# A fused attention and feed-forward block: smaller constant loads, a halved first weight load and another engine for one scaling at the start

## What is computed

```python
x = x + tanh(g_xattn[0]) * xattn(layernorm(x), ctx_2048, ...)
x = x + tanh(g_ffn[0]) * ffn(layernorm(x), ...)

# xattn: 16 query heads, 4 key/value heads of 128
q = rms_norm(x @ wq, q_norm_w)
k = rms_norm(x @ wk, k_norm_w);          v = x @ wv
k_ctx = rms_norm(h_ctx_kv @ wk_ctx, k_norm_w);  v_ctx = h_ctx_kv @ wv_ctx
q = q * cos + rotate_half(q) * sin       # k likewise, k_ctx not
scores = q @ concat([k_ctx, k]).T / sqrt(128) + causal mask on the own keys
out = softmax(scores) @ concat([v_ctx, v]) @ wo
# ffn: silu(x @ gate_w * gate_scale) * (x @ up_w * up_scale) @ down_w * down_scale,
#      weights rounded through float8_e4m3
```

## Time and profile before

| | |
|---|---|
| time before, median of 3 runs | 309.91 us (309.84 to 309.98) |
| the profiled execution | 310.24 us |
| its span in the profile | 308.0 us |
| TensorE / VectorE / ScalarE / GpSimd busy | 294.0 / 231.3 / 232.1 / 183.4 us |
| moved by DMA | 12.84 MB, most of it in the first 31 us |
| TensorE clock granted | full in all 40 slices |

### The profile page before, as it was taken

How to read it: one execution, slowest core, us unless ns; L and a number is a source line. 1 busy time by engine, 2 the same in 40 slices (tenths; PEclk the granted TensorE clock), 3 DMA queues, 4 the chain that set the end, 5 groups by cost and what they waited for, 6 DMA issues and landing times.

```text
span 308.0 us, 6587 instructions
## 1 busy us (share of the span) xinstructions
PE 294.0 (95%) x2243; PEld 235.3 (76%) x2243; DVE 231.3 (75%) x482; ACT 232.1 (75%) x893; POOL 183.4 (60%) x178
## 2 busy tenths in 40 slices
PE   7898989998999999999999999999999999988876
PEld 3345666666877888888888888888888888877865
DVE  1768997899899987879864876768765975686553
ACT  2586889977879788998887778787887678776632
POOL 1446685677648695567755685457746684556230
PEclk9999999999999999999999999999999999999999
DMA  6999000000000010001000010000000000000001
GB/s 198 388 390 397 24 17 2 0 1 10 11 3 1 2 34 2 0 2 36 2 0 2 0 37 0 3 0 20 2 1 2 0 19 2 2 0 19 0 0 36
DMA packets 6720, 12.84 MB, mean 42 GB/s; under 512 B 800, under 2 KB 4256, under 8 KB 6688
## 3 DMA queue, kind: packets, MB, share of 16 engines
q1 hardware_dynamic: 6688, 12.43, 11.3%
HBM read 11.38 MB, written 1.05 MB: 40 GB/s over the span
## 4 chain that ended last, share of the span: by engine, by line
PE 28%; ACT 28%; DVE 26%; issue 8%; POOL 5%; DMA 2%; SPq 1%; DVEq 0%; POOLq 0%
ACT probs L950 11%; ACT squares L785 6%; PE ps_y L446 4%; DVE row_max L1245 4%; DVE exp_bias L1248 4%; DVE q_sin L1109 4%; DVE q_rot L1105 3%; ACT qt L869 3%; PE ps_attn L752 3%; PE ps_scores L704 3%; ACT const L842 2%; PE ps_transposed L432 2%; PE ps_kv L420 2%; DMA q_raw<-in_wq_dram 2%; PE ps_probs L432 2%
## 5 line engine op out<-in xcount | busy, mean ns | idle before, releaser
L950 ACT ACTIVATE probs<-ps_scores,exp_bias,q_scale 128x128 f32<-128x128 f32 x128 | 56.9, 455 | 23.7 <-DVE exp_bias L1248 23.6
L1426 POOL TENSOR_TENSOR q_rot<-q_rot,q_sin 128x512 f32<-128x512 f32 x31 | 40.0, 1292 | 18.4 <-DVE q_sin L1109 18.1
L1470 POOL TENSOR_TENSOR probs<-probs,row_inv 128x512 f32<-128x512 f32 x32 | 36.2, 1133 | 17.9 <-DVE row_inv L1304 17.8
L1377 POOL TENSOR_TENSOR q_scale<-ssq_eps,minus_half 128x4 f32<-128x4 f32 x32 | 39.8, 1244 | 10.6 <-DVE ssq_eps L1274 9.6
L1388 POOL TENSOR_TENSOR fuse_lo<-fuse,fuse_hi 128x256 fp32r<-128x256 f32 x21 | 15.4, 733 | 41.3 <-ACT fuse_hi L794 41.3
L785 ACT ACTIVATE squares<-ps_q 128x128 bf16<-128x128 f32 x128 | 34.1, 292 | 5.8 <-PE ps_q L414 4.1
L752 PE MATMUL ps_attn<-pt,values 128*128 128x256 f32 x128 | 33.4, 383 | 0.0
L704 PE MATMUL ps_scores<-kt,qt 128*64 128x128 f32 x512 | 33.3, 273 | 0.0
L926 ACT ACTIVATE pt<-ps_probs 128x512 f32<-128x512 f32 x32 | 19.2, 600 | 13.3 <-PE ps_probs L432 13.3
L704 PEld LDWEIGHTS ps_scores<-kt,qt 128*64 128x64 f32 x512 | 28.9, 137 | 0.0
L1105 DVE TENSOR_TENSOR q_rot<-ps_q,rope 128x512 f32<-128x512 f32 x31 | 21.3, 686 | 9.7 <-ACT squares L785 9.7
(11 more groups left out here) (195 smaller groups left out, 839.2 us busy)
## 6 DMA issues: line engine op xcount, KB each, us to landing
q_raw<-in_wq_dram SPq DMA_DIRECT2D x4, 512.0 KB, 8.3
o_raw<-in_wo_dram SPq DMA_DIRECT2D x4, 512.0 KB, 12.3
ctx_t<-in_ctx_dram SPq DMA_DIRECT2D x8, 128.0 KB, 2.7
out_dram<-x_sb SPq DMA_DIRECT2D x8, 128.0 KB, 1.7
stage<-in_gate_w_dram SPq DMA_DIRECT2D x2, 384.0 KB, 10.1
stage<-in_up_w_dram SPq DMA_DIRECT2D x2, 384.0 KB, 11.1
x_sb<-in_x_dram SPq DMA_DIRECT2D x1, 768.0 KB, 13.1
stage<-in_down_w_dram SPq DMA_DIRECT2D x2, 384.0 KB, 13.1
```

The source lines that it names most:

```text
L950: last = nc.scalar.activation(probs[:, i, :], ps_s[:, i * P:(i + 1) * P], ACT.Exp, bias=exp_bias[:, i:i + 1], scale=q_scale[:, k % 2, i:i ...
L1377: return nc.gpsimd.tensor_tensor(dst, src, minus_half[:, 0:src.shape[1]], ALU.pow)
L1426: nc.gpsimd.tensor_tensor(q_rot[:, :, :], q_rot[:, :, :], q_sin[:, :, :], ALU.add)\
L1470: nc.gpsimd.tensor_tensor(probs[:, :, :], probs[:, :, :], row_inv[:, :].unsqueeze(2).broadcast_to([P, 4, P]), ALU.mult).then_inc(probs_rea ...
```

## The change

Six edits, all in what is done before step 0:

1. The norm weights come as two rows of 128 (`norm_w`, 128 KB over all partitions, where it was 256 KB). The swapped halves are read by an access pattern when the rope tables are made.
2. The causal mask moves from the table ahead of `q` 0 (160 KB before, 128 KB now) into `small` (7.5 KB before, 39.5 KB now), which is loaded after `q` 0. `mask_tables` waits for `small`.
3. The first weight chunk, `wk_ctx`, is loaded in two halves of 256 KB with a semaphore each, so one more DMA is issued. TensorE waits for the first half, multiplies with it, waits for the second and multiplies with that.
4. The first gate chunk is issued ahead of the fourth query chunk.
5. ScalarE scales the context keys, one instruction for each of four heads with the head's inverse root as a scale column, after the squares of the own keys. VectorE's one instruction for it is gone.
6. The own keys' inverse roots have a tile of their own, `own_inv`. GpSimd no longer waits for the scaled context keys before it writes them.

```diff
-C_COS, C_SIN, C_MASK, C_ID, C_ALL = 0, DIM, 2 * DIM, 2 * DIM + LEN, 2 * DIM + LEN + P
-S_KW, S_GATES, S_GATE, S_UP, S_ALL = 0, 1, 3, 3 + FC, 3 + 2 * FC
+C_COS, C_SIN, C_ID, C_ALL = 0, DIM, 2 * DIM, 2 * DIM + P
+S_KW, S_GATES, S_GATE, S_UP, S_MASK, S_ALL = 0, 1, 3, 3 + FC, 3 + 2 * FC, 3 + 2 * FC + LEN
...
-CHUNKS = [("kv", 0), ("kv", 1), ("q", 0), ("kv", 2), ("kv", 3), ("q", 1), ("q", 2), ("q", 3),
-          ("gate", 0), ("gate", 1), ("up", 0), ("up", 1),
+CHUNKS = [("kv", 0), ("kv", 1), ("q", 0), ("kv", 2), ("kv", 3), ("q", 1), ("q", 2), ("gate", 0),
+          ("q", 3), ("gate", 1), ("up", 0), ("up", 1),
...
-            for n in range(2):
-                load_chunk(n)
-            sp.dma_start(rope[:, :, :].rearrange("p a n -> p (a n)"),
-                         norm_rows.rearrange("(a n) -> a n", a=1).broadcast_to([P, 4 * DIM])).then_inc(rows_in, 16)
+            sp.dma_start(kv_raw[:, 0, 0, :], wk_ctx[:, 0:GW]).then_inc(first_half_in, 16)
+            sp.dma_start(kv_raw[:, 0, 1, :], wk_ctx[:, GW:2 * GW]).then_inc(chunk_in[0], 16)
+            load_chunk(1)
+            sp.dma_start(norm_w[:, :, :].rearrange("p a n -> p (a n)"),
+                         norm_rows.rearrange("(a n) -> a n", a=1).broadcast_to([P, 2 * DIM])).then_inc(rows_in, 16)
...
-                keys_values(0, -4)
+                pe.wait_ge(ctx_in_sem[0], 16)
+                pe.wait_ge(first_half_in, 16)
+                nc.tensor.matmul(kv_bank(0, 0, 0)[:, :], ctx_t[:, 0, 0, :], kv_raw[:, 0, 0, :], start=True, stop=False)
+                weights_ready("kv", 0, 0)
+                nc.tensor.matmul(kv_bank(0, 0, 0)[:, :], ctx_t[:, 0, 1, :], kv_raw[:, 0, 1, :], start=False, stop=True)\
+                    .then_inc(kv_made["k_ctx"], 1)
...
                 square_heads(kv_bank(0, 0, 1), k_ssq).then_inc(ks_squared, 1)
+                act.wait_ge(kc_inv_ready, 1)
+                for h in range(GROUPS):
+                    last = nc.scalar.activation(kn_first[:, h, :], four(kv_bank(0, 0, 0))[:, h, :], ACT.Copy,
+                                                scale=k_inv[:, h:h + 1])
+                last.then_inc(kc_ready, 1)
                 act.wait_ge(small_in, 16)
                 act.wait_ge(kc_turned, 1)
...
-                nc.vector.tensor_tensor(rope[:, n, :], const[:, col:col + DIM], rope[:, n, :], ALU.mult)\
-                    .then_inc(tables_ready, 1)
+                weights = norm_w[:, n // 2, :].rearrange("p (f j) -> p f j", f=2)
+                nc.vector.tensor_tensor(rope[:, n, :].rearrange("p (f j) -> p f j", f=2),
+                                        const[:, col:col + DIM].rearrange("p (f j) -> p f j", f=2),
+                                        weights if n % 2 == 0 else weights[:, ::-1, :], ALU.mult).then_inc(tables_ready, 1)
...
-                by_head = k_inv[:, :].unsqueeze(2).broadcast_to([P, HPG, DIM])
+                by_head = own_inv[:, :].unsqueeze(2).broadcast_to([P, HPG, DIM])
...
+                dve.wait_ge(ks_squared, 1)
                 dve.wait_ge(kc_inv_ready, 1)
-                nc.vector.tensor_tensor(kn_first[:, :, :], four(kv_bank(0, 0, 0)), by_head, ALU.mult).then_inc(kc_ready, 1)
-                dve.wait_ge(ks_squared, 1)
...
                 pool.wait_ge(ks_var_ready, 1)
-                pool.wait_ge(kc_ready, 1)
-                inverse_root(k_inv[:, :], k_var[:, :]).then_inc(ks_inv_ready, 1)
+                inverse_root(own_inv[:, :], k_var[:, :]).then_inc(ks_inv_ready, 1)
```

15 lines of the change are left out of this document (8 added, 7 removed).

## The result

The changed kernel takes 311.03 us (median of 14 runs, 310.66 to 312.13) against 309.99 us (309.81 to 310.36, 14 runs) for the kernel before: a ratio of 1.0034, 95% interval 1.0026 to 1.0042. It is slower by a third of a per cent, where the prediction had 0.18% faster and a range that ended at 310.0. The profiled execution took 311.23 us, its span is 309.5 us (before: 310.24 and 308.0). The spans of all 14 executions lie between 308.6 and 310.1 us with 309.1 in the middle, so what the trace shows is a somewhat larger loss than the usual one.

What follows compares the result with a forecast made beforehand. One hand-ordered pipeline was taken as the bound, with two nearly level chains before step 0. Their gains of 0.61 and 0.62 us, taken as 0.56, gave 309.35 us against 309.91 (-0.18%), range 308.9 to 310.0.

Steps and rivals of the forecast that it cites:

- the first of the loads: Before step 0: own-key weights, behind one more issue, land at 7.65 us instead of 7.59, at most 8.06.
- The broadcast: Loads before step 0: halved norm weights and smaller table bring the first query weights 0.9 us earlier, to 9.97.
- the loss goes by packets: Norm-weight load: 128 packets remain, so the lost 1.0 us stays; part of a rival at 309.5 to 309.7, chance 0.08.
- First weights in halves: TensorE before step 0: starts at 5.87, context keys done 0.50 us earlier at 7.85; 0.42 goes on to the own keys.
- Own-key chain: Before step 0: own keys end at 9.65, their rotation on VectorE starts at 10.93 instead of 11.54, 0.61 us earlier.
- ScalarE's four scalings: Context keys before step 0: new cost of 1.15 us, 10.85 to 12.00, with TensorE's turn of them at 12.06.
- Edits priced at nothing: Before step 0: gate chunk ahead of the fourth query chunk and mask in `small` change no time.
- The sum: Chains before step 0 give 0.61 and 0.62 us, taken as 0.56; row maxima of step 0 at 18.75, not 19.31.
- From step 0 on: Time saved before step 0 counts once, not 32 times; later work keeps its old distances on all engines.
- the slower rival: VectorE and GpSimd meet otherwise; one long `exp_bias` and `ssq_eps` more cost 1.33 us against 0.56: 310.7, chance 0.12.
- own-key weights after 7.8: Sign in the profile after: own-key weights landing later than 7.8 us would make the prediction wrong in its terms.

Runs made afterwards that it cites:

- small_first: Kernel before with its 7.5 KB table issued ahead of the first key weights instead of behind the query weights: 310.88 us against 310.11.
- merged_start: Kernel before with identity and first context tile loaded as one DMA of 192 KB, one DMA fewer: 309.76 us against 309.87.
- merged_halves: Kernel before with identity and first context tile in one DMA and the first key-weight chunk in halves: 311.21 us, +0.36%.
- constants_alone: Kernel before with only the norm weights as two rows (128 KB) and the mask moved into `small`: 310.11 us against 310.09.
- after_whole_chunk: Changed kernel with the first key weights loaded as one 512 KB chunk again, other edits kept: 309.86 us against 310.09 for the kernel before.
- gate_alone: Kernel before with only the first gate chunk issued ahead of the fourth query chunk: 309.95 us against 309.87.
- rows_replicated: Kernel before with its four norm rows stored 128 times, so each partition reads its own 2 KB: 310.05 us against 310.11.
- whole_chunk_replicated: Changed kernel with the first chunk whole and its two norm rows stored 128 times: 309.56 us against 310.11 for the kernel before, ratio 0.9986.
- scaling_alone: Kernel before with only ScalarE scaling the first context keys and a separate tile for the own keys' inverse roots: 309.87 us against 310.09.

## Why the prediction was wrong, point by point

- **The step that failed** is the first of the loads: "One more issue (0.43 us, rows 3) stands ahead of them, but the time from issue to landing grows [...], so the transfers wait for each other and not for their issue." The bounds were 7.59 and 8.06, and the landing was 9.12. Two things failed in it. The issue isn't hidden behind the other transfers: a small DMA more brings the own-key weights to 8.08 (small_first), the upper bound, and one fewer to 7.00 (merged_start). And the upper bound took the issue for the most that the edit can cost, while cutting the chunk added another 1.1 us from issue to landing (6.06 against 4.98), and 1.0 us in merged_halves, where the issue is no later than before. The growing times show that a queue exists. They don't show that its 16 engines stay together, and it was the last of them that fell behind.
- **The broadcast**: bounds 0.40 to 1.40, taken 0.9, measured 0.16 at the query weights (constants_alone) and 0.12 (after_whole_chunk), of which 0.11 is there in gate_alone with no byte changed. Even the sum of the terms that I held safe, 0.32 "in any case" and 0.08 for the table, wasn't there. With a limit by reads, bytes saved inside the slow stretch save nothing. The rival "the loss goes by packets" had the right cause and the wrong price, since it kept the 0.32. The 0.9 was there to be had at the landing, by another edit (rows_replicated).
- **First weights in halves**: TensorE starts at 5.84 (5.87 predicted) and has the context keys at 7.72 (7.85). The mechanism was right. The gain is swallowed by the wait for the next weights, 1.44 us.
- **Own-key chain**: own keys end at 11.14, not 9.65. The rotation follows at 12.44, 1.30 behind them (predicted: 10.93 - 9.65 = 1.28). So the working behind the weights holds and only its start was off.
- **ScalarE's four scalings**: 1.16 us against 1.15, right. They end at 13.36 and the turn starts at 14.21 behind the queries, so they cost nothing here; in whole_chunk_replicated they hold TensorE 0.55 us. The Trainium skill ("ScalarE: Activation LUTs", "What ACT_TABLE_LOAD costs") gives an estimate of 1.27 us by its figures; the four took 1.16 us in the kernel after and in scaling_alone, so the trace doesn't agree with it.
- **Edits priced at nothing**: right, by gate_alone.
- **The sum**: by the two rules of distance, loads at 9.97 and a rotation at 10.93 give 18.33 and 18.69, so 18.69, close to the 18.75 predicted. With the landings as they were the same rules give 12.34 + 8.36 = 20.70. The term is the loads' alone.
- **From step 0 on**: right. 1.39 us at step 0 and at step 31; the meetings of VectorE and GpSimd on which the slower rival rested didn't change. So the time came out slower (0.12) by a mechanism that I had not named, and not by that one. The prediction named its sign: own-key weights after 7.8.

## What to carry to other kernels

Where the first loads of a kernel are waited for, price an additional DMA by the landing of whatever is issued behind it: at least its issue (here 0.5 us at the next weights), 0.8 to 1.0 us further down the queue, and 1.5 to 1.9 us at the next weights where it comes of cutting a chunk in two. Before cutting a first load, try it alone. Joining two loads brought the next landing forward by 0.57 us, but no time that could be measured. A row broadcast to all partitions from one place in memory may be limited by its reads: halving its length gave nothing, while storing it once for each partition brought the landing of the query weights forward by 0.9 to 1.1 us, for more bytes in memory and none more moved. That became time (0.14%) only where the other chain was shortened as well. And with two chains that end level, write down the distance of each to the place where they meet: it sorts the later experiments at a glance.
